# Two-layer delta/latent kernel: latents and attention merged into one block, first delta chunk loaded earlier, gate weights split ahead of the tokens

## The chip, the cores and the metric

One core of one Trainium2 chip. Its engines are TensorE (PE; its weight loads are shown as PEld), VectorE (DVE), ScalarE (ACT), GpSimd (POOL) and SyncE (SP, which issues all DMAs here). The metric is the device time in microseconds of one execution.

## The reference, cut to what matters

`x` is 2 sequences of 1024 tokens of 512 features, in float32. Four sublayers, each with a residual and a layer norm ahead:

```
x = x + delta(layernorm(x))      # 6 heads of 64: q,k,v = silu(causal conv4(x W)), l2-normed q,k, gated delta rule, gated rms norm, out
x = x + nvfp4_ffn(layernorm(x))  # 4096 hidden, weights unpacked from 4-bit codes
x = x + latent_attn(layernorm(x))
x = x + sparse_ffn(layernorm(x)) # 2048 hidden, 2-of-4 sparsified

q_lat, kv_lat = x @ wq_d, x @ wkv_d              # 512 -> 64 each
q = rope(q_lat @ wq_u); k = rope(kv_lat @ wk_u)  # 16 heads of 16
v = kv_lat @ wv_u                                # 16 heads of 32
out = softmax(q k^T / 4) v @ wo                  # per head 1024 x 1024, no mask
```

## The kernel before, in words

Every float32 product is made of three fp32r products of high and low halves (`matmul3`): ACT casts a tile to its high half, DVE (or POOL) subtracts it for the low half. The program is a row of blocks. Within a block every engine has its own list of instructions, written out by hand, and semaphores order them; between two blocks all engines meet. `stream` [128, 16 tiles, 512] holds the residual for the whole run.

`project_front` (L462 to 776): tokens are loaded in four groups of four tiles, normed, turned, split and multiplied by the gate weights; ACT splits the gate weights (`gate_hi`) behind the first token tile and DVE takes `gate_lo` behind `low(0)`. Then q, k and v are projected in nine rounds (three 128-feature tiles, in each q, k, v), convolved by four taps on DVE, passed through silu on ACT and stored to the DRAM tensor `qkv`, half a round (one sequence, 512 KB) per DMA. SP waits for all stores, the block ends, and `delta_rule` starts by loading chunk 0 (`load(0)`, L907) from `qkv`.

`delta_rule` (L779): eight chunks of 128 tokens for both sequences. For a chunk, PE turns queries, keys and values, ACT makes squares, norms and the decay columns (`decay_columns`, twelve copies), PE makes `decays_between`, then `keys_by_keys`; DVE makes the triangular blocks; SP moves them by way of DRAM; POOL solves them in 62 dependent steps (L992, L997). Chunks 0 and 1 are prepared ahead of the loop. PE begins with `sum_decays`, `decays_between(0)`, `turn_queries(0)`, `turn_keys_values(0)`, `keys_by_keys(0)`.

`nvfp4_feed_forward` (L181): PE is dense. On DVE the last thing is `add` of the last four tiles to `stream`.

`latent_inputs` (L1758), a block of its own: DVE makes the statistics of all 16 tiles (first 4, then 12), scales, and takes low halves; ACT the high halves; PE turns, makes the latents (`latent`, four groups) and the values.

`softmax_heads` (L1951), the next block: for the first two of eight passes (a pass is 4 heads of one sequence) PE projects rotated queries and keys (`project`), DVE multiplies by the tables, adds and splits them, SP stores them to DRAM (`rotated`) and loads them back as `q_stack[j]`, `k_stack[j]`, 14 DMAs per head (`load`, L2021). For passes 2 to 7 one quarter of a pass is projected during each head (`project_piece`, heads 0 to 23). A head has T = 8 tiles. For a tile PE makes `query_scores`, DVE their row maxima (`maximum`), the maxima of a head are turned (`turn_top`), copied (`copy_top`) and written as one row into `q_stack` by SP (`place_top`); then PE makes `key_scores`, ACT the exponentials, PE the `output`. Query scores run AHEAD = 15 tiles ahead. Score banks are three, used in turn. The PE order of a head is fixed (L2363 and around L2385):

```
behind = ((-3,), (-2, -1), (), (0,), (1,), (2,), (3,), (4,))[t]     # output tiles made in step t
for t in range(T):
    query_scores(step + AHEAD)         # waits exp_done(step)
    if t == 1: turn_top(g + 1)
    if t == 2: project_piece(g)        # only while n + 2 < 8
    if t == 5: turn_out(g - 1)
    output(...)  for the tiles above
    key_scores(step + 1)               # waits max_done(step + AHEAD)
```

All these share the bank `turned` (turned maxima, projected piece, turned output), so each waits until the one ahead has been copied out.

Of the kernel before, what the change touches and what calls it, by code (L numbers as in the profile page):

```python
# [88 lines left out]
class Norm:  # L89

    def __init__(self, scope):
        self.raw = scope.sb("raw_stats", [P, TILES, 6])
        self.mean, self.gap, self.var, self.power, self.rstd = (
            scope.sb(x, [P, TILES]) for x in ("mean", "gap", "var", "power", "rstd"))
# [4 lines left out]
def of_sequences(ap, rows):  # L99

    return ap[:].rearrange("p (b c) -> p b c", b=BATCH)[:, :, rows]


def token_moments(dve, norm, rows, stats, group):

    at = 7 * group
    raw = norm.raw[:].rearrange("p (b c) x -> p b c x", b=BATCH)[:, :, rows, :]
    mean, gap, var = (of_sequences(x, rows) for x in (norm.mean, norm.gap, norm.var))
# [13 lines left out]
def inverse_deviation(pool, norm, rows, group):  # L122

    pool.wait_ge(norm.moments, 7 * group + 7)
    rstd, var, power = (of_sequences(x, rows) for x in (norm.rstd, norm.var, norm.power))
# [54 lines left out]
def nvfp4_feed_forward(nc, stream, ident, norm, fp4, codes, scales):  # L180
# [6 lines left out]
    with Scope(nc, "fp4") as s:  # L187
# [31 lines left out]
        @block.gpsimd  # L219
        def _(pool):  # L220
            inverse_deviation(pool, norm, LATE, 1)

# [17 lines left out]
        def _(dve):  # L240
# [30 lines left out]

            def body(it, first, last):
                for t in range(STEPS):
# [43 lines left out]
            body(LOOPS - 1, False, True)  # L317
            add(STEPS * LOOPS - 1, BLOCKS - 1)
# [125 lines left out]

def masks():
# [10 lines left out]
def project_front(nc, stream, ident, mask, hidden, ident_in, masks_in, w_qkv, conv_w, w_gate, head_rows, qkv, beta, decay,  # L456
                  fp4):
# [6 lines left out]
    with Scope(nc, "pf") as s:  # L464
# [13 lines left out]
        homes = (fp4.weight[:].rearrange("p n c -> p (n c)"), fp4.early[:], fp4.early[:, BATCH * SEQ:])  # L478
        rows = [home[:, 0:BATCH * SEQ].rearrange("p (b t) -> p b t", b=BATCH) for home in homes]
# [4 lines left out]
        arrived = [s.sem(f"arrived{q}") for q in range(BLOCKS)]  # L484
# [19 lines left out]
        def _(sp):  # L504
# [17 lines left out]
            for n in range(3 * CT):  # L522
                tile, q = divmod(n, 3)
                for b in range(BATCH):
                    sp.wait_ge(silu_done, BATCH * n + b + 1)
                    sp.dma_start(qkv[CT * q + tile][:, b * SEQ:(b + 1) * SEQ], rows[q][:, b, :]).then_inc(stored[q][b], 16)
# [3 lines left out]
            for q in range(3):  # L530
                for b in range(BATCH):
# [2384 lines left out]
```

## Time and profile before

| | us |
|---|---|
| median of 3 runs | 2858.09 (2857.4 to 2864.46) |
| the profiled execution's own time | 2853.56 |
| its span, first to last instruction | 2851.8 |
| busy: PE, DVE, ACT, POOL | 2669.8, 1645.0, 895.5, 380.0 |
| mean granted TensorE clock | 0.961 |

Times of rows are from the span's start in the profiled execution. The blocks: front to 171, delta rule to 594, NVFP4 to 1655, latents to 1710, attention to 2231, then output projection and sparse layer. PE is busy 94% of the span, so what counts is where it is not, and what it waits for there.

### The profile page before, as it was taken

The page shows a single profiled execution, that of the slowest core. Times are in us where ns is not written, and L with a number is a line of the kernel's source. Part 1 is how long each engine was busy: PE and PEld are TensorE (multiplying, and loading weights), DVE is VectorE, ACT ScalarE, POOL GpSimd, SP SyncE. Part 2 cuts the span into 40 slices and gives each one's busy share as a digit, 9 for nine tenths or more (in the row PEclk, how much of TensorE's full clock was granted, in tenths as well). Part 3 has the DMA queues.
Part 4 walks back from the last instruction along what each step waited for, and adds up shares of the span by engine and source line. Part 5 has one row for each costly group of instructions (what it writes and reads, how often), then busy time and mean ns, then how long its engine had stood idle before and what let it go on. Part 6 is the DMA issues. An engine that isn't in the chain of part 4 may idle for free. (4 is left out here: it accounts for less than half of the span.)

```text
span 2851.8 us, 34712 instructions
## 1 busy us (share of the span) xinstructions
PE 2669.8 (94%) x12842; PEld 1987.5 (70%) x12842; DVE 1645.0 (58%) x2424; ACT 895.5 (31%) x1360; POOL 380.0 (13%) x672
## 2 busy tenths in 40 slices
PE   7966898889999999999999976999999999999998
PEld 7855777868888888888888852333333678888886
DVE  6864768674544444545545356777776465645544
ACT  3442343322111111121121134666666322222221
POOL 0028767400000000000000002222210100000000
PEclk9977989989999999999999987999999999999999
DMA  2242322201100000000010002222221001000001
GB/s 90 99 128 48 76 55 60 65 30 35 32 23 22 22 22 22 22 22 22 22 36 9 1 28 94 71 76 73 70 80 35 30 16 40 35 30 15 15 15 45
DMA packets 102039, 123.44 MB, mean 43 GB/s; under 512 B 50400, under 2 KB 77280, under 8 KB 100256
## 3 DMA queue, kind: packets, MB, share of 16 engines
q1 hardware_dynamic: 101920, 121.86, 14.3%
q8 instruction: 73, 1.20, 0.2%
q14 instruction: 46, 0.38, 0.0%
HBM read 94.55 MB, written 26.74 MB: 43 GB/s over the span
## 5 line engine op out<-in xcount | busy, mean ns | idle before, releaser
L2217 DVE TENSOR_REDUCE att_top<-att_scores 128x1 f32<-128x1024 f32 x256 | 312.2, 1224 | 136.9 <-PE att_scores L2303 136.9
L284 DVE TENSOR_TENSOR fp_hidden<-fp_gelu,fp_up 128x512 f32<-128x512 f32 x128 | 88.0, 687 | 441.9 <-PE fp_up L75 379.0
L2151 ACT ACTIVATE att_probs<-att_scores 128x1024 f32<-128x1024 f32 x256 | 262.4, 1025 | 204.8 <-PE att_scores L2326 202.9
L2339 PE MATMUL att_out<-att_probs,att_padded 128*64 128x512 f32 x1024 | 269.6, 616 | 2.9 <-issue 2.8
L270 DVE TENSOR_TENSOR k_stream<-k_stream,fp_down 128x512 f32<-128x512 f32 x256 | 175.3, 685 | 89.7 <-PE fp_down L75 86.1
L343 ACT ACTIVATE fp_gelu<-fp_gate 128x512 f32<-128x512 f32 x128 | 76.4, 597 | 419.9 <-PE fp_gate L75 419.0
L73 PE MATMUL fp_gate<-fp_feat_hi,fp_w_hi 128*128 128x512 f32 x512 | 200.5, 392 | 4.9 <-DVE fp_feat_lo L258 4.9
L75 PE MATMUL fp_gate<-fp_feat_hi,fp_w_lo 128*128 128x512 f32 x512 | 199.9, 391 | 0.0
L74 PE MATMUL fp_gate<-fp_feat_lo,fp_w_hi 128*128 128x512 f32 x512 | 199.9, 390 | 0.0
L73 PE MATMUL fp_down<-fp_w_hi,fp_h_hi 128*128 128x512 f32 x512 | 199.3, 389 | 0.0
L75 PE MATMUL fp_up<-fp_feat_hi,fp_w_lo 128*128 128x512 f32 x512 | 199.2, 389 | 0.0
L73 PE MATMUL fp_up<-fp_feat_hi,fp_w_hi 128*128 128x512 f32 x512 | 199.2, 389 | 0.0
L75 PE MATMUL fp_down<-fp_w_hi,fp_h_lo 128*128 128x512 f32 x512 | 199.2, 389 | 0.0
L74 PE MATMUL fp_down<-fp_w_lo,fp_h_hi 128*128 128x512 f32 x512 | 199.2, 389 | 0.0
L74 PE MATMUL fp_up<-fp_feat_lo,fp_w_hi 128*128 128x512 f32 x512 | 199.2, 389 | 0.0
L2326 PEld LDWEIGHTS att_scores<-att_q_stack,att_k_stack 64*128 64x128 f32 x512 | 48.0, 185 | 186.5 <-issue 129.9
L2625 DVE TENSOR_TENSOR la_values<-la_values,sp_up 128x512 f32<-128x512 f32 x64 | 44.0, 688 | 224.2 <-PE sp_up L75 223.3
L1819 POOL MEMSET lat_power<- 128x16 f32 x1 | 0.1, 112 | 1049.8 <-POOLq L52 1049.8
L997 POOL TENSOR_TENSOR f_blocks<-f_blocks,dr_base_tmp 48x31 f32<-48x31 f32 (+15 forms) x248 | 135.7, 547 | 19.4
L328 ACT CAST fp_w_hi<-f_weight 128x1536 fp32r<-128x1536 f32 x32 | 47.1, 1476 | 289.2 <-DVE f_weight L165 279.6
L992 POOL TENSOR_TENSOR dr_base_tmp<-f_blocks 48x31 f32<-48x31 f32 (+15 forms) x248 | 124.4, 502 | 89.4 <-DMA f_blocks<-blocks_l 70.3
L2326 PE MATMUL att_scores<-att_q_stack,att_k_stack 64*128 64x512 f32 x512 | 127.7, 497 | 1.6 <-DVE att_top L2217 1.6
(330 smaller groups left out, 5641.8 us busy)
## 6 DMA issues: line engine op xcount, KB each, us to landing
f_early<-codes SPq DMA_DIRECT2D x16, 768.0 KB
f_early<-scales SPq DMA_DIRECT2D x16, 768.0 KB
att_q_stack<-rotated SPq DMA_DIRECT2D x192, 64.0 KB, 2.6
att_k_stack<-rotated SPq DMA_DIRECT2D x192, 64.0 KB, 2.7
la_values<-w_sparse SPq DMA_DIRECT2D x10, 1024.0 KB, 4.9
f_early<-qkv SPq DMA_DIRECT2D x16, 576.0 KB, 6.1
qkv<-f_early SPq DMA_DIRECT2D x12, 512.0 KB, 2.9
k_stream<-hidden SPq DMA_DIRECT2D x4, 1024.0 KB, 10.6
```

What stands on the lines that cost most here:

```text
L73: pe.matmul(out, w_hi, x_hi, start=start, stop=False)
L74: pe.matmul(out, w_hi, x_lo, start=False, stop=False)
L75: return pe.matmul(out, w_lo, x_hi, start=False, stop=stop)
L270: dve.tensor_tensor(tile, tile, down_ps[j][:], ALU.add).then_inc(added, 1)
L284: dve.tensor_tensor(hidden[:, c, :], gelu[:, c, :], up_ps[c][:], ALU.mult).then_inc(product_done, 1)
L343: act.activation(gelu[:, c, :], gate_ps[c][:], ACT.Gelu_apprx_tanh).then_inc(gelu_done, 1)
L992: pool.tensor_tensor(update, base_l[rows, j, j + 1:].unsqueeze(2).broadcast_to(shape), base_t[rows, j, 0:done].unsqueeze(1).broadcast_to(s ...
L997: pool.tensor_tensor(target, target, update, ALU.subtract).then_inc(base_step, 1)
L2151: act.activation(probs[:, tile % PROBS, :], key_bank(tile)[:], ACT.Exp).then_inc(exp_done, 1)
L2217: dve.tensor_reduce(top[g % 2][:, STACK + t:STACK + t + 1], query_bank(tile)[:], AX.XY, ALU.max, negate=True).then_inc(max_done, 1)
L2326: last = pe.matmul(key_bank(tile)[:, half, :], k_stack[j][rows, t * P:(t + 1) * P], q_stack[j][rows, half * TB:(half + 1) * TB], start=Tru ...
L2339: last = pe.matmul(out[rows, :], padded[:, g % 2, t, :], probs[:, t, half * TB:(half + 1) * TB], start=t == 0, stop=t == T - 1)
```

## The change

1. Start: the first group of tokens comes in two DMAs of two tiles, with a semaphore each (`first_in`, `arrived[0]`); the gate weights are loaded ahead of the identity; ACT makes `gate_hi` ahead of `high(0)`, DVE `gate_lo` ahead of `low(0)`.
2. Convolved queries go to columns 384 to 511 of `stream` (eight runs of 512 bytes per partition), keys to `fp4.weight`, values to the part of `fp4.early` behind the first chunk's place. Before the stores of the last value round SP waits for all query and key stores and loads the queries and keys of chunk 0; behind the value stores it loads chunk 0's values. In `delta_rule` PE no longer waits at its start for DVE's three constants; it turns queries, keys and values first and makes `decays_between(0)` behind them; ACT makes the squares ahead of `decay_columns(0)`, and its table is loaded at the end of the front. The front's semaphores are given back with those of the delta rule.
3. NVFP4: DVE takes the statistics of 12 of the 16 tiles in the last steps (`next_stats`) and two groups of moments, one group of four and all of the second ahead of the last `add`; POOL the powers.
4. `latent_inputs` and `softmax_heads` become `latent_attention`, one block: one hand-written order of turning, latents, projections of the two prepared passes (in halves of 512 tokens), and values. POOL takes the weights' low halves, the rotated sums and their low halves. The two prepared passes are loaded from SBUF directly (12 DMAs for the first four heads), the row of ones by DMA. Features live in half of their former space, the second half of it in `stacks`.
5. In the heads: AHEAD is 13, and the steps of the bank `turned` move: `turn_top` and `copy_top` t = 1 to 3, `project_piece` 2 to 4, `copy_piece` 3 to 4, `high_piece` 6 to 7, `turn_out` and `normalise_head` 5 to 6. The table of output tiles per step stays. `load` has 10 DMAs instead of 14 (the high and low rows of one copy in one).

The diff, cut to its core:

```diff
@@ nvfp4_feed_forward, vector
+            def next_stats(n, t):
+                dve.wait_ge(added, SUB * (n + 2))
+                for i in tiles_of(t):
+                    dve.bn_stats(norm.raw[:, i, :], stream[:, i, :]).then_inc(norm.stats_done, 1)
...
+                    if last and b == 1 and tb >= 2:
+                        next_stats(n - 2, tb - 2)
...
             body(LOOPS - 1, False, True)
+            token_moments(dve, norm, EARLY, TILES + 2 * SUB, 2)
+            next_stats(STEPS * LOOPS - 2, 2)
+            token_moments(dve, norm, LATE, TILES + 3 * SUB, 3, FIRST)
             add(STEPS * LOOPS - 1, BLOCKS - 1)
@@ project_front, sync
-            load_tokens(0)
+            load_first(0)
+            load_first(1)
+            sp.dma_start(gate_w[:], w_gate.rearrange("k p n -> p k n")).then_inc(gate_w_in, 16)
             sp.dma_start(ident[:], ident_in).then_inc(ident_arrived, 16)
-            sp.dma_start(gate_w[:], w_gate.rearrange("k p n -> p k n")).then_inc(gate_w_in, 16)
...
+                if n == 3 * CT - 2:
+                    for part in range(2):
+                        for b in range(BATCH):
+                            sp.wait_ge(stored[part][b], 16 * CT + 16)
+                    for b in range(BATCH):
+                        load_first_rows(b, slice(0, 2 * CT), first_qk_in)
...
+            for b in range(BATCH):
+                sp.wait_ge(stored[2][b], 16 * CT + 16)
+                load_first_rows(b, slice(2 * CT, 3 * CT), first_v_in)
@@ project_front, scalar and vector
-            high(0)
             act.wait_ge(gate_w_in, 16)
             act.copy(gate_hi[:], gate_w[:]).then_inc(gate_hi_done, 1)
+            high(0)
...
-            low(0)
             dve.wait_ge(gate_hi_done, 1)
             dve.tensor_tensor(gate_lo[:], gate_w[:], gate_hi[:].bitcast(F32), ALU.subtract).then_inc(gate_lo_done, 1)
+            low(0)
@@ delta_rule, tensor and scalar
             sum_decays()
-            decays_between(0)
             for c in range(2):
                 turn_queries(c)
-                turn_keys_values(c)
                 if c:
-                    decays_between(c)
+                    turn_keys_values(c)
+                else:
+                    turn_first_keys()
+                    turn_first_values()
+                decays_between(c)
                 keys_by_keys(c)
...
-            decay_columns(0)
             exponents()
-            exponent_of_decays(0)
             for c in range(2):
                 square_queries(c)
                 square_keys(c)
+                if c == 0:
+                    decay_columns(0)
                 norm_logs(c)
-                if c:
-                    exponent_of_decays(c)
+                exponent_of_decays(c)
@@ latent_attention
-AHEAD = 2 * QTILES - 1
+AHEAD = 2 * QTILES - 3
...
+            for i in range(4):
+                scale(i)
+            for i in range(4):
+                low_feats(i)
+                scale(i + 4)
+            low_feats(4)
+            low_feats(5)
+            low_latent(0)
...
+            for i in range(6):
+                turn(i)
+            latent(0)
+            turn(6)
+            turn(7)
+            project(0)
+            latent(1)
+            turn(8)
+            turn(9)
+            project(1)
+            value(0)
...
+            project(3)
+            latent(3)
+            for i in range(QTILES, TILES):
+                value(i)
             for tile in range(AHEAD):
                 query_scores(tile)
...
-                    if t == 1 and g + 1 < HEADS:
+                    if t == 3 and g + 1 < HEADS:
                         turn_top(g + 1)
-                    if t == 2 and has_piece(g // QUAD):
+                    if t == 4 and has_piece(g // QUAD):
                         project_piece(g)
-                    if t == 5 and g:
+                    if t == 6 and g:
                         turn_out(g - 1)
```

## Rows read from the trace of the kernel before

**Rows 1.** Windows by block: PE, PEld, DVE, ACT, POOL busy, PEclk, DMA share, GB/s.

```profile
1655.00:1710.00 55.00, 36.66 (x160) 26.96 (x160) 33.94 (x70) 22.79 (x39) 3.77 (x3) 0.81 0.11 36
1710.00:1749.00 39.00, 16.81 (x55) 8.80 (x55) 27.65 (x27) 11.84 (x12) 9.53 (x12) 0.65 0.33 109
1749.00:2231.00 482.00, 472.05 (x2321) 165.97 (x2321) 325.20 (x342) 297.18 (x340) 81.12 (x126) 0.99 0.22 65
```

**Rows 2.** Timeline of the start: start, duration, engine, line, operation, idle before.

```profile
6.53 2.47 DVE L618 BATCH_NORM_STATS2 pf_raw_stats<-k_stream 128x6 f32<-128x512 f32 x4 [6.53 <-DMA k_stream<-hidden]
...
13.40 1.51 ACT L585 CAST pf_gate_hi<-pf_gate_w 128x1584 fp32r<-128x1584 f32 x1
...
14.94 1.81 DVE L687 TENSOR_TENSOR pf_gate_lo<-pf_gate_w,pf_gate_hi 128x1584 fp32r<-128x1584 f32 x1 [0.72 <-ACT pf_gate_hi L585]
...
18.03 0.68 PE L73 MATMUL pf_gate<-pf_gate_hi,pf_feat_hi 128*128 128x396 f32 x1
```

**Rows 3.** Timeline between the front and the first blocks of the delta rule.

```profile
161.89 2.95 ACT L567 ACTIVATE f_early<-f_early 128x1024 f32<-128x1024 f32 x3
...
162.98 5.20 SPq L526 DMA_DIRECT2D qkv<-f_early  x4
...
171.00 1.02 SPq L910 DMA_DIRECT2D f_early<-qkv  x2
...
175.96 2.07 PE L1050 MATMUL dr_bank<-dr_g_cols,l_mask 128*128 128x512 f32 x2 [1.59 <-ACT dr_g_cols L1279]
...
186.51 3.60 ACT L1279 ACTIVATE dr_g_cols<-l_mask,da_decay 128x128 f32<-128x128 f32 x12
...
189.82 4.20 PE L1061 MATMUL dr_bank<-f_early 64*128 64x128 f32 x24 [5.99 <-DVE dr_k_d L1506]
...
201.38 0.23 POOL L992 TENSOR_TENSOR dr_base_tmp<-f_blocks 48x31 f32<-48x31 f32 x1 [26.02 <-DMA f_blocks<-blocks_l]
```

**Rows 4.** POOL's start on the second chunk.

```profile
239.23 0.24 POOL L992 TENSOR_TENSOR dr_base_tmp<-f_blocks 48x31 f32<-48x31 f32 x1 [0.27 <-POOL f_blocks L997]
```

**Rows 5.** DMA issues: KB each, median us from issue to landing.

```profile
f_early<-qkv SPq DMA_DIRECT2D x16, 576.0 KB, 6.1
qkv<-f_early SPq DMA_DIRECT2D x12, 512.0 KB, 2.9
lat_wu<-w_up SPq DMA_DIRECT2D x1, 512.0 KB, 6.0
```

**Rows 6.** Timeline from NVFP4's last addition to the first query and key scores.

```profile
1649.15 0.69 DVE L270 TENSOR_TENSOR k_stream<-k_stream,fp_down 128x512 f32<-128x512 f32 x1 [0.67 <-PE fp_down L75]
...
1654.59 0.69 DVE L270 TENSOR_TENSOR k_stream<-k_stream,fp_down 128x512 f32<-128x512 f32 x1 [0.67 <-PE fp_down L75]
...
1661.85 3.67 PE L1918 MATMUL lat_turned<-k_ident,lat_normed 128*128 128x128 f32 x16 [7.29 <-DVE lat_normed L1874]
...
1731.10 1.65 PE L2303 MATMUL att_scores<-att_k_stack,att_q_stack 64*128 64x512 f32 x6 [13.74 <-DMA att_q_stack<-att_k_stack]
...
1749.35 0.79 PE L2326 MATMUL att_scores<-att_q_stack,att_k_stack 64*128 64x512 f32 x2 [1.56 <-DVE att_top L2217]
```

**Rows 7.** Groups of instructions; the third in the attention's POOL work.

```profile
L1879 DVE TENSOR_TENSOR lat_feat_lo<-lat_turned,lat_feat_hi 128x512 fp32r<-128x512 f32 x16 | 10.7, 687 | 12.6 <-ACT lat_feat_hi L1834 12.6
L1874 DVE TENSOR_SCALAR lat_normed<-k_stream,lat_mean,lat_rstd 128x512 f32<-128x512 f32 x16 | 8.2, 537 | 0.0
L2101 POOL TENSOR_TENSOR att_piece_lo<-att_piece,att_piece_hi 128x256 fp32r<-128x256 f32 x24 | 17.6, 734 | 77.3 <-ACT att_piece_hi L2139 77.3
```

**Rows 8.** PE in head 9 (with a piece): step 1, then projection.

```profile
1888.38 1.94 PE L2339 MATMUL att_out<-att_probs,att_padded 128*64 128x512 f32 x8
...
1890.91 0.39 PE L73 MATMUL att_turned<-la_lat_hi,la_up 128*128 128x256 f32 x1
```

**Rows 9.** PE in a head without a piece: the query scores behind an empty step 2.

```profile
2131.07 0.51 PE L2303 MATMUL att_scores<-att_k_stack,att_q_stack 64*128 64x512 f32 x2 [0.65 <-ACT att_probs L2151]
```

**Rows 10.** PE's waits from 1780 to 2228: total, times, longest.

```profile
PE att_scores L2303 <- ACT att_probs L2151: 3.9, 6, 0.7
```

More of the change, by code:

```diff
@@ L1963, in softmax_heads @@
         out, turned = s.ps("out", [P, TB]), s.ps("turned", [P, TB])
-        product = scores[1:]
+        turned_ps = [scores[b // 2][:, b % 2, :].rearrange("p (k t) -> p k t", k=KT) for b in range(4)]
+        ring, val_ps = [scores[2][:, b, :] for b in range(2)], (out[:], turned[:])
         rot_hi, rot_lo = s.sb("rot_hi", [P, PREPARED, SEQ], F32R), s.sb("rot_lo", [P, PREPARED, SEQ], F32R)
@@ new lines, in high_rotated @@
+            def high_rotated(k):
+                n, half = divmod(k, 2)
+                at = slice(half * TB, (half + 1) * TB)
+                act.wait_ge(rot_done, k + 1)
+                if n:
+                    act.wait_ge(lat_done, BLOCKS)
+                    act.wait_ge(val_done, TILES)
+                act.copy(rot_hi[:, n, at], rot[:, n, at]).then_inc(rot_hi_done, 1)
+            for i in range(SUB):
+                high_feats(i)
+            act.wait_ge(down_in, 32)
+            act.copy(wd_hi, wd32).then_inc(w_hi_done, 1)
@@ L2185, in _ @@
         def _(dve):
-            for copy in COPIES:
-                dve.memset(ones[top_row(copy), :], 1.0).then_inc(ones_done, 1)
-            for b in range(2):
-                dve.memset(top[b][:], 0.0).then_inc(blank_done, 1)
-            dve.wait_ge(blank_done, 2)
-            def multiply(n, x):
-                dve.wait_ge(proj_done, 2 * n + x + 1)
-                dve.tensor_tensor(part[:, 2 * n + x, :], product[x][:].rearrange("p a t -> p (a t)"),
-                                  tables[:, x, :], ALU.mult).then_inc(part_done, 1)
@@ new lines, in multiply @@
+            def multiply(k):
+                half = k % 2
+                if k == 0:
+                    dve.wait_ge(tables_in, 16)
+                if k >= 2:
+                    dve.wait_ge(rot_done, k - 1)
+                for x in range(2):
+                    dve.wait_ge(proj_done, 2 * k + x + 1)
+                    dve.tensor_tensor(part[:, k % 2, x * TB:(x + 1) * TB], ring[RING[k][x]],
+                                      tables[:, x, half * TB:(half + 1) * TB], ALU.mult).then_inc(part_done, 1)
@@ new lines, in latent @@
+            def latent(b):
+                if b == 0:
+                    pe.wait_ge(w_lo_done, 1)
+                pe.wait_ge(feat_lo_done, SUB * (b + 1))
+                if b:
+                    pe.wait_ge(part_done, (0, 1, 3, 7)[b])
+                hi, lo = feats[b % 2][:, 0], feats[b % 2][:, 1]
+                for kt in range(KT):
+                    last = matmul3(pe, ring[b % 2], wd_hi[:, kt, :], wd_lo[:, kt, :],
+                                   hi[:, kt, :], lo[:, kt, :], kt == 0, kt == KT - 1)
+                last.then_inc(lat_done, 1)
@@ L2357, in outputs_of_step @@
                 return [T * g + tile for tile in behind if T * g + tile >= 0]
[L2359 to L2363 removed]
+            for i in range(6):
[9 more added lines that the diff above has]
+            value(0)
+            value(1)
+            turn(10)
+            turn(11)
+            value(2)
+            value(3)
+            latent(2)
+            project(2)
+            turn(12)
+            turn(13)
+            value(4)
+            value(5)
+            turn(14)
+            turn(15)
+            value(6)
+            value(7)
+            project(3)
+            latent(3)
+            for i in range(QTILES, TILES):
+                value(i)
             for tile in range(AHEAD):
```

601 lines of the change are left out of this document (327 added, 274 removed).

## The prediction

> **What bounds the kernel now.** I read the windows by block first. They show a dense PE in the attention heads (472 of 482 us) and two thin stretches ahead of them: 55 us of latents with PE busy for 36.7, and 39 us up to the first key scores with PE busy for 16.8 at a mean granted clock of 0.65 [rows 1]. Next the timelines of the places that the change touches. At the start, PE's gate products wait until 18.03 for a chain on ACT and DVE [rows 2]. Between the front and the delta rule PE waits, and with it POOL, whose first dependent step comes at 201.38, 30.4 us after the block began at 171.00 [rows 3]. POOL goes from chunk 0 straight on to chunk 1 [rows 4], and everything after hangs on that chain, so a shift of POOL's start passes on whole. Last, the order of the heads on PE: where its list has nothing between two score products, it waits for ACT [rows 9, 10].
>
> **The change part by part.** All sums are against the profiled execution's 2853.56; its difference is then put on the median, 2858.09.
>
> *Start.* The gate split now stands ahead of the first token tile. Before: statistics of four tiles end at 9.0, `gate_hi` runs 13.40 to 14.91, `gate_lo` 14.94 to 16.75, products from 18.03 [rows 2]. After: two of the four statistics are done before the second half lands, so moments come about 1.2 earlier (half of 2.47) and scaling ends near 10.8. `gate_hi` can run while DVE works on moments, so `gate_lo` takes 10.8 to 12.6. `low(0)` (0.7), `scale(2)` (0.5) and one turn at the low clock (0.9) follow: products from 14.8. Gain 3.2. If the gate weights land later than about 9 it shrinks: bounds 1 and 3.5. Behind that the front is PE's, so the gain passes on.
>
> *End of the front.* Relative to the old times: the second key store is issued at about 164.0 and lands at 166.9 (2.9 [rows 5]). SP then issues two loads of 384 KB (about 0.5 each, from 1.02 for two [rows 3]), and only then the first value store (was 165) and the second (was 167.9). What is queued behind this wait on SP is the value stores, and the block's end waits for them. The loads take 786 KB at the pace of the old ones (576 KB in 6.1 with two in flight, about 250 KB per us: 3.0), the stores 1.3 each. If the stores go behind the loads, the last lands near 173.7 instead of 170.7, plus 0.5 for issuing the last load of values: the block ends at 174.2, 3.2 later. If they pass beside them only the issues count: 0.6. I take 3.2, as in the old trace the four stores too came one behind the other. The Trainium skill (DMA: Bandwidth & Descriptors, Queues, rings and completion order) says that on each DMA engine descriptors are consumed in ring order. By that the late end is the right one; no row here separates the two.
>
> *Delta rule, chunk 0.* Before, the keys' products begin 18.8 after the block (189.82 less 171.00), waiting for DVE's values and keys, which came after late turns [rows 3]. After, with the data there: `sum_decays` to 1.8, queries turned to 3.2, keys to 4.5, ACT's squares to 5.2, the columns to 8.8 (3.6 [rows 3]), norms to 9.3, DVE's refinement and four products to 12.5 (as 186.4 to 189.8), PE's decays 8.9 to 14.0 (they began at 175.96 and took 5). Keys' products begin at 14.0: gain 4.8. The values, issued just ahead of the block's end, land near 3 and are not late. Bounds: 2 (the decays now wait behind the values) and 8 (the first load no longer counts). So the front and this together: 3.2 less 3.2 plus 4.8, a gain of 4.8.
>
> *End of NVFP4.* DVE is idle in the last steps, but eight statistics (two fours of 2.47 [rows 2]) and two groups of moments (0.9 each) now stand between the fifth last and the last four additions. DVE is free from 1649.8, when the fifth last addition ends; 1649.8 plus 2.5, 0.9, 2.5, 0.9 is 1656.6, then four additions of 0.65: 1659.3 instead of 1655.3 [rows 6]. Loss 4.0.
>
> *The merged block.* I walked the five lists by hand with durations from the rows: low half 0.67, scaling 0.51 on DVE (busy by count [rows 7]), POOL 0.73 per 256 elements [rows 7], so 1.5 for 512. The first latent waits for POOL (memset of 3.8, then the split): 7.2. ACT waits for `wu` (6.0 to land [rows 5], so 7.2), casts it and tiles 4 and 5: 9.4. Then the chain goes: POOL's split of `wu` 11.1, low latent 13.9, `project(0)` 15.4, multiplications 17.4, `latent(1)` 19.7, its low half 21.2, the last statistics and moments 24.6. From there DVE leads: tiles 8 to 11 to 31, `latent(2)` 33.9, its split, `project(2)` and multiplications to 37.6, tiles 12 to 15 to 42.1, `project(3)`, `latent(3)` 46.2, values 8 to 15 (eight of 0.7 and waits for ACT's copies) 52.6. DVE's work alone is 10.7 + 8.2 + 2.7 + 5.4 + 3.5 = 30.5. PE's turns come without the old gap of 7.3, so its clock may rise sooner (16 turns took 3.67 at the low level [rows 6]); that takes 2.4 off. I take 51.4 from the block's start. The stacks are filled before: rotated halves at 30.5, 24 DMAs of 0.45, landed by 44. The same walk for the old block ends within 0.3 of the trace. Thirteen maxima instead of 15: 18.25 between first query and first key scores [rows 6], less 2 of 1.14, is 16.0. The row of maxima is in place 2 us earlier, behind 12 DMAs on SP. From last addition to key scores: 0.3 + 51.4 + 16.0 = 67.7, before 94.1 [rows 6]. Gain 26.4, with the loss of 4.0: 22.4. Bounds: 17 (the two halves of the walk each 10% long) and 26.
>
> The Trainium skill (GPSIMD Engine Reference, Elementwise) gives GpSimd about twice VectorE's time for a float32 sum of two tensors, which speaks against moving the splits to POOL. The row's 734 ns for 256 against 687 for 512 on DVE is worse than that; POOL's slack here, 7 us ahead of the loads, covers either.
>
> *The heads.* Before, step 2 of heads 0 to 23 holds the projection between two pairs of score products (0.75 from 1890.91) and PE never waits. Heads 24 to 29 have an empty step 2: the next query scores must wait until ACT has cleared a bank, 0.65 each, six times [rows 9, 10]. The change moves the projection to step 4, where PE already has an output tile, and leaves step 2 empty in all heads. So 24 heads more take this wait: 24 x 0.65 = 15.6. The two query products taken out of the start come back here, 0.7. Loss 16.3. The loads' shorter list on SP and the later placing of the row (needed four steps on, ready after about two) hide behind PE. Bounds: 0 if something fills the step, 20 if `turn_top` waits 0.1 more for a maximum in every head.
>
> Sum: -4.8 - 22.4 + 16.3 = -10.9. Profiled 2842.7, median 2847.
>
> **The rivals.**
> - *The hole in step 2 costs nothing.* For it: PE's list is otherwise as long, ACT is busy 62% only. Against it: six waits of 0.65 with the same neighbours [rows 10]. Time: 2858.1 - 27.2 = 2831.
> - *The merged block gives half.* Its engines hand over to each other far more often, and statistics and ACT's wait for `wu` stand in front of others. If the walk is 10 us short: 2857, no change. Against it: the same walk fits the old block.
> - *Slower: the projection waits for the turned row.* In step 1 two outputs (1.94 [rows 8]) stood between `turn_top` and the projection, in step 3 only one. DVE's maximum (1.23) and copy (0.29) would no longer be covered, if they start late. It decides from 1.1 us per head on (27.2 over 24). With one whole output, 0.97, on top of 0.65 it is 38.9 in place of 15.6: 2870. Against it: by the walk the copy is done 0.4 ahead of PE.
>
> **How the numbers follow.** My forecast has 0.60, the free hole 0.10, the short gain 0.21, the slower case 0.09. Forecast: 2847, own range 2840 to 2855, from the front's bounds (2 to 9 in all), the block's and the heads'. About 0.3% (8.6 us) is what a measurement of this kernel can tell from no change; that is 2849.5. Of the forecast 0.45 lies below it, so faster is 0.45 + 0.10 + 0.01 = 0.56, same 0.15 + 0.19 = 0.34, slower 0.09 + 0.01 = 0.10. The range goes from the free hole to just short of the slower case: 2831 to 2861.
>
> **What would show it.** After: gate products near 14.8; POOL's first step near 196.6; the last addition of NVFP4 about 4 us further behind its last product; key scores about 68 us behind that addition; in PE's waits on ACT `att_scores` 30 waits of about 0.65 instead of 6. Wrong would be: no such waits, a DMA ahead of the first query scores, `turn_top` or the projection waiting for DVE by more than 0.3, or the first value store landing as early as before.

## The result, and the profile after

| | us |
|---|---|
| median after, 4 runs | 2836.76 (2834.59 to 2840.83) |
| median before, 4 runs | 2857.74 (2854.86 to 2864.46) |
| ratio, 95% interval | 0.9927 (0.9913 to 0.994) |
| profiled execution after, its span | 2840.83, 2839.0 |

The change makes the kernel 21 us faster; the forecast was 2847, 11 below 2858.09. The time lies within the forecast's outer range (2831 to 2861) and 3 us below the narrower one (2840 to 2855). The direction was right. The stages show that the reason was another one.

**The ledger.** Each stage is measured from the first instruction that marks it to the next, on PE, in the profiled executions:

| us | before | after | difference | forecast |
|---|---|---|---|---|
| start to first product of NVFP4 | 601.57 | 595.63 | -5.9 | -4.8 |
| last down product of NVFP4 to first query scores | 76.9 | 60.8 | -16.1 | -20.1 |
| to first key scores | 18.2 | 16.3 | -1.9 | -2.3 |
| to the last turned output (heads) | 480.3 | 505.4 | +25.1 | +16.3 |
| sparse layer, from its first product | 550.4 | 537.2 | -13.2 | 0 |
| the rest (NVFP4, output projection) | | | -0.6 | 0 |

The sum is -12.6, and the spans differ by 12.8; the rest is rounding. So all that the forecast spoke of adds up to nothing here, and the profiled gain is that of a layer which the change does not touch. The medians differ by 8 more. The profiled execution of before was quicker than all four timed beside it and that of after was its slowest, and the delta rule by itself is not repeatable to that: from GpSimd's first step to NVFP4's first product it took between 393 and 407 us over twelve traces, with no relation to what was edited. Kernels with the same code in a stage repeat to 0.4 in the merged block, to 0.6 in the sparse layer, and to 3 in the heads (their waits for the row differ); the two traces with the old blocks of latents and attention's start are 1.6 apart there. I therefore rest on stages wherever an effect is under 10 us.

**Start of the changed kernel**, timeline, answers to [rows 2]:

```profile
4.63 2.63 DVE L665 BATCH_NORM_STATS2 pf_raw_stats<-k_stream 128x6 f32<-128x512 f32 x4 [4.63 <-DMA k_stream<-hidden]
...
8.09 1.51 ACT L628 CAST pf_gate_hi<-pf_gate_w 128x1584 fp32r<-128x1584 f32 x1 [6.06 <-DMA pf_gate_w<-w_gate]
...
10.27 1.80 DVE L733 TENSOR_TENSOR pf_gate_lo<-pf_gate_w,pf_gate_hi 128x1584 fp32r<-128x1584 f32 x1
...
13.95 0.68 PE L73 MATMUL pf_gate<-pf_gate_hi,pf_feat_hi 128*128 128x396 f32 x1
```

The half load lands 1.9 us earlier than the whole one did, which I had not counted; products begin at 13.95.

**From front to delta rule**, timeline after, answers to [rows 3]:

```profile
163.46 0.96 SPq L544 DMA_DIRECT2D f_early<-qkv  x2
...
164.46 1.01 SPq L564 DMA_DIRECT2D qkv<-f_early  x2
169.94 1.59 SPq L544 DMA_DIRECT2D f_early<-qkv  x2
171.99 1.38 POOL L1028 MEMSET dr_diag<- 128x1536 f32 x1 [133.00 <-POOLq L52]
...
176.78 3.60 ACT L1344 ACTIVATE dr_g_cols<-l_mask,da_decay 128x128 f32<-128x128 f32 x12
...
186.86 2.37 PE L1126 MATMUL dr_bank<-f_early 64*128 64x128 f32 x24
...
197.75 0.23 POOL L1041 TENSOR_TENSOR dr_base_tmp<-f_blocks 48x31 f32<-48x31 f32 x1 [21.40 <-DMA f_blocks<-blocks_l]
```

The value stores stand behind two loads and land at 169.9 and 171.2; the block ends 7.7 behind ACT's last silu, where it ended 3.2 behind [rows 3]. Keys' products start 14.9 behind the block's start, where it was 18.8.

**NVFP4's end and the merged block**, timeline after, answers to [rows 6]:

```profile
1643.01 0.69 DVE L279 TENSOR_TENSOR k_stream<-k_stream,fp_down 128x512 f32<-128x512 f32 x1 [0.67 <-PE fp_down L75]
...
1650.20 2.47 DVE L279 TENSOR_TENSOR k_stream<-k_stream,fp_down 128x512 f32<-128x512 f32 x4
...
1653.54 3.68 POOL L2061 MEMSET att_stacks<- 128x4096 f32 x1
...
1653.68 3.81 DVE L2212 TENSOR_SCALAR att_probs<-k_stream,k_mean,k_rstd 128x512 f32<-128x512 f32 x1
...
1708.80 0.47 PE L2411 MATMUL att_scores<-att_stacks 64*128 64x512 f32 x1
...
1725.11 0.80 PE L2436 MATMUL att_scores<-att_stacks 64*128 64x512 f32 x2 [1.56 <-DVE att_top L2254]
```

A scaling that takes 0.54 elsewhere takes 3.81 here: it runs until GpSimd's clearing is over.

**Windows after**, columns as in [rows 1]: the block as a whole, the heads, and two stretches of the block:

```profile
1653.00:1709.00 56.00, 43.99 (x184) 31.78 (x186) 33.09 (x57) 23.76 (x41) 23.25 (x16) 0.87 0.29 64
...
1725.00:2231.00 506.00, 473.56 (x2325) 168.36 (x2325) 326.92 (x341) 297.29 (x340) 80.91 (x126) 0.99 0.21 61
```

```profile
1664.00:1679.00 15.00, 11.64 (x55) 8.45 (x53) 9.24 (x22) 5.63 (x10) 5.06 (x4) 1.00 0.00 0
1679.00:1689.00 10.00, 7.68 (x23) 5.44 (x24) 5.21 (x9) 2.86 (x5) 5.17 (x6) 0.66 0.29 46
```

PE's granted clock falls again in the middle of the block, behind the turns that wait for DVE: it is at its low level (half, 1.2 GHz) from 1681.5 to 1688.3. The products from 1683.0 to 1688.2 run at that level, one in 0.43 us instead of 0.23.

**PE's waits in the heads after**, answers to [rows 10]: total, times, longest:

```profile
PE att_scores L2411 <- ACT att_probs L2126: 21.7, 30, 0.7
PE att_scores L2436 <- DMA att_stacks<-att_top_rows: 6.9, 13, 1.2
```

The 30 waits are the forecast ones. The 13 others, of the key scores for the row of maxima, are new.

**The sparse layer**, PE in the same window before, after, and in the first experiment. The number in brackets counts matmuls; PE is busy throughout and at full clock in all three.

```profile
2400.00:2500.00 100.00, 100.00 (x432) 1.00 0.09 32
```

```profile
2400.00:2500.00 100.00, 100.00 (x443) 1.00 0.09 32
```

```profile
2400.00:2500.00 100.00, 100.00 (x443) 1.00 0.09 32
```

One matmul every 0.2315 us before, every 0.2257 after (turns included). By the starts of neighbours it is 0.2333 before and 0.2267 after in gate and up, and 0.2307 and 0.2267 in down. This time from one start to the next is called the pitch below. A busy share of 100% hides it.

### The profile page after: what moved, and what is told of

The parts are those of the page before. It is cut to its first block and busy times, and to the rows that moved or that the text cites. A ratio compares the mean times of both kernels' runs of the same rounds, so it can differ in the third digit from the quotient of the medians.

```text
span 2839.0 us, 34635 instructions
## 1 busy us (share of the span) xinstructions
PE 2653.1 (93%) x12842; PEld 1985.8 (70%) x12842; DVE 1639.9 (58%) x2426; ACT 886.7 (31%) x1354; POOL 395.2 (14%) x678
## 5 line engine op out<-in xcount | busy, mean ns | idle before, releaser
L2436 PEld LDWEIGHTS att_scores<-att_stacks 64*128 64x128 f32 x512 | 48.2, 185 | 193.2 <-issue 93.7
L133 POOL TENSOR_TENSOR k_rstd<-k_var,k_power 128x8 f32<-128x8 f32 (+1 forms) x7 | 10.2, 1459 | 1133.8 <-DVE k_var L126 1133.7
L2436 PE MATMUL att_scores<-att_stacks 64*128 64x512 f32 x512 | 125.6, 487 | 8.9 <-DMA att_stacks<-att_top_rows 6.9
```

Source lines behind the costliest of these rows:

```text
L2436: last = pe.matmul(key_bank(tile)[:, half, :], k_stack[j][rows, t * P:(t + 1) * P], q_stack[j][rows, half * TB:(half + 1) * TB], start=Tru ...
```

## Experiments

Ratios are to the kernel before, timed beside each; the stages are those of the ledger. e1 to e4 were timed together, e5 to e8, and e9 to e12.

**e1, addresses alone.** On the kernel before:

```diff
     with Scope(nc, "la") as keep:
+        kept = keep.sb("kept", [P, 11, TILES])
         values = keep.sb("values", ...)
...
-            norm = Norm(f)
+            norm = Norm(f, kept)      # its tensors lie in kept
```

> The kernel before, with nothing moved but addresses: 704 bytes are taken ahead of the latent sublayers' tensors, so that these and the sparse layer's weights lie where the changed kernel has them (the weights at 116032 instead of 115328; the features stay at 148800). Theory A: the sparse layer's faster matmuls in the changed kernel (one every 0.2267 us instead of 0.2333) come from the addresses; then that pitch shows here too and the time falls by about 13 us, to 0.9955 of the kernel before. Theory B: it was the chip or the execution; then the pitch stays at 0.2333 and the time is within 3 us of the kernel before.

Measured: 2843.45, 0.9957 (0.9944 to 0.997); sparse layer 537.7, its pitch 0.2267. That is theory A: addresses alone give 12 us. The change had moved one `Norm` from the top of the memory to the bottom, and with it everything between by 704 bytes.

**e2, 64 bytes further.** The changed kernel with `keep.sb("pad", [P, 16])` ahead of `values`.

> The changed kernel, with 64 bytes taken ahead of the latent sublayers' tensors: in the sparse layer both operands of the matmuls of gate and up now start 128 bytes above a multiple of 256 (64 above before). If it counts that both lie alike, the pitch stays at 0.2267 and the time at 0.9927 of the kernel before. If it counts that an operand starts at 64 above, the pitch goes to 0.2333 and the time to about 0.9975. If addresses mean nothing, no change either.

Measured: 2840.48, 0.9945 (0.993 to 0.996); sparse layer 537.5, 443 matmuls in 100 us. So the pitch does not need a start at 64 bytes above a multiple of 256; with both operands alike it is fast here too. The whole kernel is 3 us under e1, timed beside it.

**e3, the row first.** On the changed kernel, SP's list in the heads:

```diff
+                if g + 1 < HEADS:
+                    place_top(g + 1)
                 if g and g + QUAD - 1 < HEADS:
                     ...
                     (load_prepared if to < PREPARED else load)(to, slot)
-                if g + 1 < HEADS:
-                    place_top(g + 1)
```

> The changed kernel, with the row of maxima issued ahead of the next head's ten loads instead of behind them. Theory A: the row is late because it stands behind the loads in the rings; the 13 waits of the key scores for it (6.9 us) go, and the time falls by about 6, to 0.9905 of the kernel before. Theory B: the row's own latency sets it, and the waits stay. Against the gain: loads issued some 5 us later could be late for their query scores; then waits of query scores for a DMA appear and the time does not fall.

Measured: 2903.31, 1.0171 (1.0154 to 1.0187); heads 567.0. PE's waits in the heads:

```profile
PE att_scores L2411 <- DMA att_stacks<-att_stacks: 50.8, 21, 4.3
```

No key score waits for the row any more, so theory A was right about the place, and useless: the loads behind it are late by up to 4.3 us, 21 times. PE's idle time in the heads grew by 31 us, half of the 61.6 by which they became longer. The rest is its clock: with these holes the granted clock of the heads fell from 0.99 to 0.92, and the same matmuls kept PE busy 30 us longer (473.56 in the changed kernel).

```profile
1726.00:2293.00 567.00, 503.87 (x2321) 0.92 0.19 54
```

The order had no slack to give; I had written this down as "against" and priced it at nothing.

**e4, the old steps in the heads of the changed kernel.**

```diff
-AHEAD = 2 * QTILES - 3
+AHEAD = 2 * QTILES - 1
-                    if t == 3 and g + 1 < HEADS:       # turn_top, copy_top
+                    if t == 1 and g + 1 < HEADS:
-                    if t == 4 and has_piece(g // QUAD):   # project_piece
+                    if t == 2 and has_piece(g // QUAD):
-                    if t == 6 and g:                   # turn_out, normalise_head
+                    if t == 5 and g:
```

with `copy_piece` in step 3 and `high_piece` in step 6.

> The changed kernel with the steps of before in the heads: query scores 15 tiles ahead, maxima turned in step 1, projection in step 2, outputs turned in step 5. My theory: the empty step 2 costs 24 x 0.65 = 15.6 and the late row 6.9; both go, and the two more maxima ahead of the first head cost 2.3 less the two query products of 0.7. So about 20 us faster than the changed kernel: 0.9855 of the kernel before. Rival: the heads' 25 us come from something else (the loads' shorter list, the high and low halves' places); then the heads stay at about 505 us from first key scores to the last turned output and the time at 0.993.

Measured: 2815.2, 0.9858 (0.9844 to 0.9873), as forecast; heads 479.5, query to key scores 19.1. PE's waits for ACT in the heads:

```profile
PE att_scores L2410 <- ACT att_probs L2126: 4.1, 7, 0.7
```

**e5, the hole alone.** e4, but projection and its copy in step 4, the high half in step 7, turned outputs in step 6.

> As e4 (query scores 15 tiles ahead, maxima turned in step 1), but the projection stays in step 4 and the turned outputs in step 6, so step 2 is empty in all heads and the row of maxima is early. It parts the heads' 25 us into two: by my theory the 30 waits of 0.65 for ACT are back (15.6 above e4) and the waits for the row are not: 0.9912 of the kernel before. Rival: the late row and the hole are one cost (the one hides in the other); then it stands at 0.9927, as the changed kernel.

Measured: 2844.34, 0.9965 (0.9953 to 0.9978), where 0.9912 was expected; heads 506.5. The hole's waits are back. So are those for the row, which I had expected to go:

```profile
PE att_scores L2410 <- ACT att_probs L2126: 18.9, 29, 0.7
PE att_scores L2435 <- DMA att_stacks<-att_top_rows: 7.7, 12, 1.6
```

SP's list and PE in one head of e5:

```profile
1864.57 0.34 SPq L1981 DMA_DIRECT2D rotated<-att_piece_hi  x1
...
1865.83 0.65 SPq L1958 DMA_DIRECT2D att_stacks<-rotated  x1
...
1871.62 1.40 SPq L1976 DMA_DIRECT2D att_stacks<-att_top_rows  x2
```

```profile
1866.74 0.30 PE L2422 MATMUL att_turned<-k_ident,att_top 128*72 128x128 f32 x1
...
1880.64 0.50 PE L2435 MATMUL att_scores<-att_stacks 64*128 64x512 f32 x2 [0.40 <-DMA att_stacks<-att_top_rows]
```

The maxima are turned at 1866.74, but the row is issued at 1871.62, behind the loads, and these began only when the piece had been stored. PE is released by it 9.0 us after its issue, 14.8 after the first load. In the changed kernel it is 14.9 (1885.00 to 1899.92), though the row was issued at 1892.01 there, 7.9 before. So the row comes with the loads, and not at a fixed time behind its own issue.

The loads themselves take longer than before. In this head they start at 1885.62 in the kernel before and at 1885.00 in the changed one. PE, its clock, DMA share and GB/s, first before and then after:

```profile
1890.00:1895.00 5.00, 5.00 (x28) 1.00 0.28 81
1895.00:1900.00 5.00, 5.00 (x28) 1.00 0.00 0
```

```profile
1890.00:1895.00 5.00, 5.00 (x27) 1.00 0.20 68
1895.00:1900.00 5.00, 4.84 (x26) 1.00 0.09 37
```

Both lists move 776 KB. By the packets' times fourteen loads and the row are through about 9 us after the first issue (8.0 to 9.7 in all but two heads), ten loads and the row about 14 us after it, in every kernel that has the ten. So two things make the row late: when the loads start, which e9 tests, and how long they take, which no run changed by itself.

**e6, the clearing later.** On the changed kernel:

```diff
-            pool.memset(stacks[:, 0:QUAD, :].bitcast(F32), 0.0).then_inc(zeroed, 1)
             low_weights(0, wd_lo, wd32, wd_hi)
             low_weights(1, wu_lo, wu32, wu_hi)
             pool.wait_ge(w_lo_done, 2)
+            pool.memset(stacks[:, 0:QUAD, :].bitcast(F32), 0.0).then_inc(zeroed, 1)
+            pool.wait_ge(zeroed, 1)
```

> The changed kernel, with GpSimd's clearing of the first four stacks (128x4096, 3.68 us) moved from the start of the merged block behind the low halves of the weights. Theory A: while it runs, DVE's second scaling cannot (3.81 us instead of 0.54) and PE stands 2.6 us for it; moved, both go and the first query scores come about 3 us earlier: 0.9917 of the kernel before. Theory B: the weights' path (loads, ACT's cast, GpSimd's low half at 1661.6) sets the first latent anyway; then less than 1 us is won.

Measured: 2840.05, 0.9954 (0.994 to 0.9968). By the ratios that is slower than the changed kernel (0.9927), while by the traces it is 1.5 us shorter; the two were not timed side by side, and such ratios are not good to 0.003. By the stages: 59.3 to the first query scores instead of 60.8. The four scalings now take 2.13 together instead of 5.40:

```profile
1651.26 2.13 DVE L2213 TENSOR_SCALAR att_probs<-k_stream,k_mean,k_rstd 128x512 f32<-128x512 f32 x4 [0.32 <-PEq L52]
```

The lock (theory A's mechanism) is shown: with the clearing moved away, no scaling is held up. Its price at that place is theory A's too. From the first scaling to the first latent product it is 7.1 us instead of 9.9, and the lead of 2.8 stays through the next 24 us of PE's list. So theory B is refuted. Half of the lead is lost further on: the low spell of the clock in the middle of the block lasts 10.2 us instead of 6.8, and 18 products instead of 12 run in it. PE, its clock, DMA share and GB/s in 10 us of e6, where the changed kernel has a clock of 0.66:

```profile
1677.00:1687.00 10.00, 9.56 (x24) 0.51 0.45 71
```

That leaves 1.5. e10 and e11, with the same edit, have a low spell of 10.2 too. The Trainium skill (SBUF — State Buffer, Who interferes with whom) says that VectorE's `tensor_scalar` in a two-port mode and any GpSimd instruction exclude each other for a whole instruction. The trace agrees, at 3.81 us for a scaling of 0.54 beside a clearing of 3.68.

**e7, the old front.** The changed kernel with `project_front` and `delta_rule` of before, word for word.

> The changed kernel with the front and the delta rule of before: no early gate split, no early load of chunk 0. It gives the value of these two parts together. By the traces GpSimd's first step comes 3.6 us earlier with them (197.75 against 201.38), and my forecast was 4.8; so this kernel should be 3.6 to 4.8 slower than the changed one: 0.994 to 0.9945 of the kernel before. Rival: the end of the delta rule, 5.9 earlier in the changed kernel, shows the real value; then 0.995.

Measured: 2851.05, 0.9986 (0.9977 to 0.9996), where 0.994 to 0.995 was expected, and 11 us above e6, timed beside it; 1.5 of these are e6's own. GpSimd's first step, the mark that the delta rule's own scatter does not reach, comes at 203.31. Over the three traces with the old front it is 201.4 to 203.3, mean 202.5; over the eight with the changed one (e10's apart, which differs there) 195.4 to 197.8, mean 196.4. By this mark the two parts are worth 6.1, more than the 3.6 to 4.8 expected. The other 3 of the 11 are not explained; the scatter of the delta rule is larger than that.

**e8, the pitch by itself.**

```diff
+for a in range(8):              # weights at 32 * a above a multiple of 256
+    for b in range(8):          # moving operand at 32 * b
+        for i in range(24):
+            pe.matmul(banks[i % 2][:], still[a][:, 0:P], moving[b][:, 0:512], start=True, stop=True)
```

> Not the reference's computation: it copies the input to the output and multiplies constants. 64 stretches of 24 matmuls (128x128 by 128x512, float32r, each with its own weight load), one stretch for each pair of places of the two operands above a multiple of 256 bytes, 0 to 224 in steps of 32. Theory A: what counts is whether both operands lie alike; then stretches with equal places run at one every 0.2267 us and the others at 0.2333. Theory B: what counts is that the features (moving) start at 64 and the weights at 64 or 128; other patterns then appear. If all 64 are equal, the address alone is not the cause and it needs the other engines' traffic.

Weights at 32 (`sb`), moving operand at 32, 64, 96 (`mb` to `md`); the next start less this one is the time of 24:

```profile
94.42 5.63 PE L41 MATMUL bank<-mb,sb 128*128 128x512 f32 x24
99.89 5.77 PE L41 MATMUL bank<-mc,sb 128*128 128x512 f32 x24
105.49 5.67 PE L41 MATMUL bank<-md,sb 128*128 128x512 f32 x24
110.99 5.77 PE L41 MATMUL bank<-me,sb 128*128 128x512 f32 x24
```

That is 5.47, 5.60, 5.50. Sixteen of the 64 pairs are fast, 0.227 to 0.229 each, and 48 slow, about 0.233: fast are just those whose moving operand lies 0 or 64 bytes above the weights, modulo 256. No other engine works here. Theory A was half of it; the pairs at 64 were not foreseen.

**e9, one step earlier for the high half.** On the changed kernel:

```diff
-                    if t == 7 and has_piece(n):
+                    if t == 6 and has_piece(n):
                         high_piece(g)
```

> The changed kernel, with one number changed: ACT makes the piece's high half in step 6 instead of 7. In e5 the row of maxima was turned in step 1 and was still late 12 times (7.7 us), so the step of the turning is not what makes it late. Theory A: SP takes its list in order, the stores of a piece wait for its halves, the next head's ten loads stand behind the stores, and the row lands with the loads, about 14 us after their first issue; one step earlier, the waits for the row (6.9 us) nearly go: heads 499 us instead of 505, 0.9903 of the kernel before. Theory B: what makes it late is the projection's place in step 4 as such (the copy, GpSimd's rotation): then the high half waits for GpSimd, the stores go no earlier, and the waits stay.

Measured: 2833.27, 0.9917 (0.9904 to 0.9931); heads 497.5, and in PE's waits no row for the row of maxima is left:

```profile
PE att_scores L2411 <- ACT att_probs L2126: 21.6, 29, 0.7
```

That is theory A: one number takes 7.9 us off the heads, where the waits had been 6.9.

**e10, the hole filled at 13 ahead.** On the changed kernel, with e6's edit:

```diff
-                    if t == 3 and g + 1 < HEADS:          # turn_top, copy_top
+                    if t == 4 and g + 1 < HEADS:
-                    if t == 4 and has_piece(g // QUAD):   # project_piece
+                    if t == 2 and has_piece(g // QUAD):
-                    if t == 4 and has_piece(n):           # copy_piece
+                    if t == 3 and has_piece(n):
-                    if t == 7 and has_piece(n):           # high_piece
+                    if t == 6 and has_piece(n):
@@ project_piece(k), turn_top(g): the bank's users change places
-                pe.wait_ge(top_copied, k + 2)
+                pe.wait_ge(top_copied, k + 1)
-                if g >= 2 and has_piece((g - 2) // QUAD):
-                    pe.wait_ge(piece_copied, g - 1)
+                if g and has_piece((g - 1) // QUAD):
+                    pe.wait_ge(piece_copied, g)
@@ project_front
+        s.sb("pad", [P, 32])
         w32 = [s.sb(f"w32_{q}", [P, KT * P]) for q in range(3)]
```

> The changed kernel with four edits: query scores still 13 ahead, but projection in step 2 and maxima turned behind it in step 4, the piece copied in step 3 and its high half in step 6; GpSimd's clearing of the stacks behind the weights' low halves (as e6); 128 bytes ahead of the front's weights, so that they and the features both start at 64 above a multiple of 256. By the stages so far: heads 505.4 to about 481 (-24.5), merged block -1.5, front -1 to -2.5 (432 matmuls by 0.0058 if PE sets its pace): 0.983 of the kernel before, and some 2 us below e4. Rival: turned in step 4, the row is late again, 5 to 10 us.

Measured: 2808.72, 0.9829 (0.9815 to 0.9844): 48 us below the kernel before, and 0.990 of the changed one by the two ratios, within 0.002. Heads 477.8, to the first query scores 59.3, to the first key scores 16.3, and:

```profile
PE att_scores L2413 <- ACT att_probs L2128: 4.6, 7, 0.7
```

The front's products now come every 0.2267 instead of 0.2324, and GpSimd's first step comes at 193.85, 2.5 below the mean of the others and 1.5 below the lowest of them: PE did set the front's pace. The heads gave 27.6 for the forecast 24.5, and the rival is refuted: no wait for the row is left, though the loads still take 14 us.

**e11, e4 with e6's edit.**

> e4 (15 ahead, the steps of before) with the clearing of e6: e4 less 1.5 us, 0.9853 of the kernel before. Against e10 it shows whether 13 ahead (two maxima less before the first key scores, 19.1 to 16.3 us) is worth having once step 2 is filled.

Measured: 2820.54, 0.9871 (0.9855 to 0.9888), 12 above e10, timed beside it. Heads 480.8, to the key scores 18.5 instead of 16.3. By stages the heads' start gives e10 2.2, the heads 3.0 and the front about 3. So 13 ahead is worth having once step 2 is filled: the 2.2 at the start are not given back in the heads. The other 4 are not explained; five runs of e10 alone lie 13 apart.

**e12, the pitch of the sparse layer's own pairs.** The products of gate and down with the addresses of before and of after, alone on the chip:

> Not the reference's computation: constants are multiplied and the input is copied out. Thirteen stretches of 48 matmuls, twice, the second time beside 240 VectorE sums: the sparse layer's products of gate and of down at the addresses of before and of after, and simple pairs. From e8: a pair is fast (0.227) where the moving operand lies 0 or 64 bytes above the weights, modulo 256, and slow (0.233) where not. So gate at the addresses of before slow and of after fast, in both passes. Down at the addresses of before has moving data at 128 and weights at 128, 128, 64: by the rule all fast, but the kernel before showed 0.2308. If this stretch is slow here too, the rule needs the order of the weights; if it is slow only beside VectorE, it needs traffic.

First pass, gate before, gate after, down before, down after. A short matmul starts 0.03 us ahead of each stretch and ends the one before; the last row here is one of these:

```profile
94.78 11.44 PE L81 MATMUL bank<-part 128*128 128x512 f32 x48
...
106.08 11.17 PE L81 MATMUL bank<-part 128*128 128x512 f32 x48
...
117.12 11.32 PE L81 MATMUL bank<-part 128*128 128x512 f32 x48
...
128.31 11.15 PE L81 MATMUL bank<-part 128*128 128x512 f32 x48
139.29 0.19 PE L79 MATMUL bank<-part 128*128 128x64 f32 x1
```

That is 11.27, 11.01, 11.16 and 10.98 us. Gate is slow and then fast, as the rule has it. Down at the addresses of before lies between, though each of its pairs is fast by itself; with its third weights at 128 as well it took 11.01. So where the weights change places from one matmul to the next, the rule of e8 is not enough; what the full one is stays open. Beside 240 sums on VectorE the stretches took the same within 0.02. With the pitches of the sparse layer itself, 1536 x 0.0066 + 768 x 0.0041 = 13.3, and the layer became 13.2 shorter. With the differences of e12, 0.0054 and 0.0038, it would be 11.2, so the addresses by themselves give most of it.

## Why the prediction was right, and where it was wrong

*The sum.* The forecast was -4.8 - 22.4 + 16.3 = -10.9. By the same marks it became -6.1 - 18.1 + 25.1 = +0.9. Beside it stand -13.2 for which the forecast had no term. So "faster" came true by luck: the addresses, which the change moved without meaning to, gave what the forecast had expected of its own parts. The medians say the same where they were taken side by side: e2, which is the changed kernel but for 64 bytes, is 3 us under e1, which has the addresses alone (0.9945 against 0.9957, each within about 0.0015). That is no difference clear of noise.

*Start.* 3.2 forecast, 4.1 measured (13.95). The term that was off: I took half of the statistics off the wait, and not that half a load lands 1.9 earlier.

*End of the front.* The value stores did go behind the loads: the first, issued at 164.46, landed at 169.93, 5.5 later instead of 2.9 [rows 5]. This step is confirmed, and with it the order of the ring as against passing beside. 3.2 forecast, 4.5 measured. The term that was off is the loads' time. The prediction's "about 250 KB per us" does not follow from [rows 5]: two times 576 KB in 6.1 us is 189, by which the two loads take 4.2 us and not 3.0. Measured were 5.3 from the landing of the last key store (163.38) to that of the second load (168.66), for about 4 with the issues.

*Delta chunk 0.* The keys' products began 14.9 behind the block's start, for 14.0 forecast. GpSimd's first step was forecast at 196.6 and came at 196.4 in the mean. That the two agree is luck in part, since without the parts it comes at 202.5 in the mean and not at 201.38: the trace of before was a quick sample.

*End of NVFP4.* The last addition came 3.5 further behind the last product, for 4.0 forecast.

*The merged block.* From the last addition to the key scores it took 72.4, for 67.7 forecast. The thirteen maxima are right (16.3 for 16.0). The term that was mis-sized is the walk up to the first query scores: 56.1 where 0.3 + 51.4 was forecast, 4.4 too short. Two steps of it failed. The clearing "3.8, then the split: 7.2" was walked as GpSimd's alone, while it also stops DVE: the first latent came at 9.9, and at 7.1 in e6, where the clearing stands later. And the 2.4 for a clock that would rise sooner was given back. It did rise, at 1661.0, 8 us into the block instead of 22, but it fell again behind the turns that wait for DVE's second wave of scalings, and some 12 products ran at the low level, by 0.2 each 2.4. In e6 that spell was longer, by 1.3. No run took it away, so this price is read from the traces.

*The heads.* The 30 waits came as forecast, at 0.7 each. e4, e5 and e10 show that they belong to the empty step 2: they go when the projection stands there, with 15 or 13 tiles ahead. The step that failed is "The loads' shorter list on SP and the later placing of the row (needed four steps on, ready after about two) hide behind PE". The row was priced from the turning, while it hangs on SP's list. `high_piece` in step 7 delays the stores, these the loads, these the row (e9, one number, 7.9 us). I had listed the step's move in the change and given it no queue to be late in. And the shorter list is not quicker: ten loads are through about 14 us after the first issue, where fourteen took about 9. With 9, the row in the head shown, issued 7.0 us behind the first load and needed 14.8 behind it, would have been in time; that is an estimate, and a kernel with the fourteen loads and the other steps of the change was not tried. It is also why the order in e3 had no slack.

*The rivals.* The free hole is refuted (e4, e5). That the merged block gives half was too little: it gave 18.1 of 22.4. The slower case did not come: the projection never waited for DVE by more than 0.3.

## What to carry to other kernels

Count matmuls in a window, not busy time: where PE is 100% busy, its pitch can still be 3% off, and a change that moves an allocation can move it. Give each pair of operands the same address modulo 256, and compare a change with a kernel that has its addresses. When a step moves, follow what it issues through the in-order queue to the last thing behind it: a number one too high in ACT's list cost 8 us by way of two stores, ten loads and two rows of 4 KB. When DMAs are merged, look at when their data is through and not at their number. And before removing an operation between two others, ask what waited behind it for free.

## What the runs showed of the hardware

- Back-to-back float32r matmuls (128x128 weights by 512 columns) at full clock take 0.227 to 0.229 or 0.233 us, by where the two operands start in a partition (e8), with nothing else running; with weights at mixed places it lies between (e12). The Trainium skill (SBUF — State Buffer, Who interferes with whom) says that PE never waits on anyone, and that its port for weights and its port for the moving operand are independent. For VectorE, the only engine tried, e12 agrees with the first: its sums disturb nothing. That the two streams do not disturb each other is not what e8 shows, and there the measurement decides.
- Two DMAs of 4 KB issued behind ten loads on the same queue are there 9.0 us later (e5), with the loads; issued ahead of them they are in time and the loads are late (e3). The Trainium skill (DMA: Bandwidth & Descriptors, Queues, rings and completion order) has descriptors consumed in ring order on each DMA engine; the trace agrees.
- 776 KB in four loads of 128 KB, four of 64 and two of 4 were through about 14 us after the first issue, in twelve of 64 KB and two of 4 after about 9 (changed kernel and before). In the head shown under e5 the pace was 68 GB/s and then 37, against 81 and then none. Why was not tried.
- The delta rule's part of this kernel took 393 to 407 us in twelve executions while the others repeated to 3 us or better. Its granted clock is below full (0.89 to 0.93 between 235 and 560). The two longest, 407 and 404 (e10, e11), have 0.89 and the two shortest, 393 and 394 (e9, e5), 0.92 and 0.93. The time and the clock go together; which of them moves the other was not shown.
- With holes of up to 4.3 us in the heads (e3) the granted clock fell from 0.99 to 0.92, and that cost about as much as the holes.
